# One call instead of two for the second query tile's scores in a fused attention and mixture-of-experts kernel

## What is computed

```python
att = jnp.einsum('bhqd,bhkd->bhqk', q, k) * jnp.float32(SCALE)
allowed = _sliding_window_mask(t, W)          # (j <= i) & (j >= i - window + 1)
att = jnp.where(allowed[None, None], att, jnp.float32(-jnp.inf))
att = jax.nn.softmax(att, axis=-1)
out = jnp.einsum('bhqk,bhkd->bhqd', att, v)
...
x = _layernorm(x + _L0_attn_ref(x, L0_attn_w_qkv, L0_attn_w_out), axis=-1)
x = _layernorm(x + _L0_ffn_ref(x, ...), axis=-1)
```

## Time and profile before

| | |
|---|---|
| median of 3 runs | 224.28 us (223.73 to 225.29) |
| the profiled execution, its own time | 223.83 us |
| its span, first to last instruction | 221.8 us |
| around the span | 2.0 us |
| PE busy / weight loads | 203.4 us (92%) / 135.9 us |
| DVE busy | 182.9 us (82%) |
| ACT busy | 116.7 us (53%) |
| POOL busy | 89.2 us (40%) |
| mean granted TensorE clock | 0.960 |

### The profile page before, as it was taken

How to read it: one execution, slowest core, us unless ns; L and a number is a source line. 1 busy time by engine, 2 the same in 40 slices (tenths; PEclk the granted TensorE clock), 3 DMA queues, 4 the chain that set the end, 5 groups by cost and what they waited for, 6 DMA issues and landing times.

```text
span 221.8 us, 5963 instructions
## 1 busy us (share of the span) xinstructions
PE 203.4 (92%) x1906; PEld 135.9 (61%) x1908; DVE 182.9 (82%) x522; ACT 116.7 (53%) x270; POOL 89.2 (40%) x166
## 2 busy tenths in 40 slices
PE   7786999989999999999999999989999899999960
PEld 4332446555565565565566566656688798989950
DVE  6664655789979989989989998977899888988883
ACT  2200106647557557557557566769445756374530
POOL 7230003375445635635635536478244211422103
PEclk9997559999999999999999999999999999999996
DMA  4947751542633533533533431000000001000011
GB/s 113 282 117 240 202 148 46 151 147 77 170 120 104 163 110 99 162 104 99 160 104 99 158 104 29 5 26 3 0 4 0 0 3 45 7 24 24 3 47 47
DMA packets 20391, 19.66 MB, mean 89 GB/s; under 512 B 1609, under 2 KB 17937, under 8 KB 20369
## 3 DMA queue, kind: packets, MB, share of 16 engines
q1 hardware_dynamic: 20180, 19.30, 29.4%
q10 hardware_dynamic: 189, 0.09, 0.1%
HBM read 13.94 MB, written 5.24 MB: 86 GB/s over the span
## 4 chain that ended last, share of the span: by engine, by line
PE 63%; DVE 17%; issue 7%; ACT 4%; DMA 4%; POOL 1%; SPq 1%; DVEq 1%; POOLq 0%; ACTq 0%
PE bank L1051 12%; PE bank L1043 9%; PE bank L960 7%; PE bank L977 5%; PE bank L992 4%; PE bank L955 3%; PE bank L942 3%; PE bank L945 3%; PE bank L926 3%; PE bank L1089 3%; DMA ks<-k_scratch 2%; DVE rest L671 2%; DVE neg_max L748 2%; PE bank L978 2%; DVE parts L676 2%
## 5 line engine op out<-in xcount | busy, mean ns | idle before, releaser
L474 ACT ACTIVATE probs<-bank 128x384 f32<-128x384 f32 x128 | 60.0, 496 | 34.7 <-PE bank L978 32.5
L432 POOL TENSOR_SCALAR_AFFINE_SELECT probs<-probs 128x1024 f32<-128x1024 f32 x32 | 35.7, 1116 | 67.8 <-ACT probs L474 67.8
L813 DVE SCALAR_TENSOR_TENSOR x_rows<-bank,gate_c,x_rows 128x128 f32<-128x128 f32 (+1 forms) x128 | 36.6, 343 | 5.3 <-PE bank L1051 4.2
L748 DVE TENSOR_REDUCE neg_max<-bank 128x2 f32<-128x384 f32 x64 | 33.5, 546 | 3.4 <-PE bank L960 3.1
L1051 PE MATMUL bank<-w_out_sb,hid 128*128 128x128 f32 x256 | 34.2, 277 | 1.0 <-DVE x_rows L813 1.0
L1051 PEld LDWEIGHTS bank<-w_out_sb,hid 128*128 128x128 f32 x256 | 32.6, 191 | 3.4 <-DVE x_rows L813 1.4
L574 ACT ACTIVATE hid<-bank,b_in_sb 128x512 f32<-128x512 f32 x32 | 21.9, 687 | 22.4 <-PE bank L1043 22.3
L977 PE MATMUL bank<-qs,ks 75*128 75x256 bf16 x128 | 33.4, 279 | 0.1
L743 DVE TENSOR_REDUCE neg_max<-bank 128x4 f32<-128x512 f32 x32 | 21.9, 685 | 8.8 <-PE bank L945 8.1
L978 PE MATMUL bank<-qs,ks 75*128 75x128 bf16 x128 | 26.9, 218 | 0.0
L436 POOL TENSOR_SCALAR_AFFINE_SELECT probs<-probs 128x512 f32<-128x512 f32 x32 | 24.2, 756 | 0.0
(11 more groups left out here) (117 smaller groups left out, 343.8 us busy)
## 6 DMA issues: line engine op xcount, KB each, us to landing
qs<-q_scratch SPq DMA_DIRECT2D x16, 288.0 KB
ks<-k_scratch SPq DMA_DIRECT2D x16, 288.0 KB
q_scratch<-parts SPq DMA_DIRECT2D x8, 192.0 KB, 2.1
k_scratch<-parts SPq DMA_DIRECT2D x8, 192.0 KB, 2.4
x_cols<-x_t SPq DMA_DIRECT2D x8, 128.0 KB, 2.6
x_rows<-x SPq DMA_DIRECT2D x8, 128.0 KB, 2.2
k_scratch<-parts SPq DMA_DIRECT2D x8, 128.0 KB, 2.3
out<-y_sb SPq DMA_DIRECT2D x8, 128.0 KB, 1.8
```

What stands on the lines that cost most here:

```text
L432: pool.affine_select(out=own, in_=own, compare_op=ALU.is_ge, fill=0.0, base=0, pattern=[[0, 2], [0, 4], [1, P]], channel_multiplier=-1).th ...
L474: nc.scalar.activation(probs[g][:, :, i, :], st_banks(spare)[k % len(st_banks(spare))][:, 0:3 * P].rearrange("p (k c) -> p k c", k=3), ACT ...
L748: nc.vector.tensor_reduce(neg_max[:, 1, 4 * g + 2 * u:4 * g + 2 * u + 2], score_bank[1 + u][:, 0:384].rearrange("p (h c) -> p h c", h=2), ...
L813: nc.vector.scalar_tensor_tensor(token_rows(c, n), y_bank[e % 4][:, n * E:(n + 1) * E], gate_of(c, n, e), token_rows(c, n), ALU.mult, ALU. ...
```

## The change

The function takes both u at once. It issues both waits and both mask products, then all eight 64-column products. It stands where the call for u = 0 stood, ahead of `turned_scores` i = 1; the call for u = 1, ahead of `turned_scores` i = 2, is gone. Number and form of the products are the same as before.

```diff
-            def scores_second_tile(b, g, u, in_use):
+            def scores_second_tile(b, g, in_use):
 
                 q, k = qs[b.parity][g // 2], ks[b.parity][g // 2]
-                bank_u = score_bank[1 + u]
-                if in_use:
-                    pe.wait_ge(maxima, b.times(3 * QUADS, 3 * g - (1 - u)))
-                edges = bank_u[:, 0:384].rearrange("p (h a c) -> p h a c", h=2, a=3)[:, :, 0:3:2, :]
-                mm(edges, ident_bf[:, :], mask_second[:, :, :].unsqueeze(1).to_broadcast([P, 2, 2, 64]), start=True, stop=True)
-                for i in range(2):
-                    h = 4 * (g % 2) + 2 * u + i
-                    for half in range(2):
-                        lo = 64 * half
-                        last = mm(bank_u[lo:lo + 64, i * 192:(i + 1) * 192], q[0:ROWS, h, P + lo:P + lo + 64], k[0:ROWS, h, lo:lo + 192],
-                                  start=False, stop=True, skip_group_check=True)
-                last.then_inc(scores_ready, 1)
+                for u in range(2):
+                    if in_use:
+                        pe.wait_ge(maxima, b.times(3 * QUADS, 3 * g - (1 - u)))
+                    edges = score_bank[1 + u][:, 0:384].rearrange("p (h a c) -> p h a c", h=2, a=3)[:, :, 0:3:2, :]
+                    mm(edges, ident_bf[:, :], mask_second[:, :, :].unsqueeze(1).to_broadcast([P, 2, 2, 64]), start=True, stop=True)
+                for u in range(2):
+                    for i in range(2):
+                        h = 4 * (g % 2) + 2 * u + i
+                        for half in range(2):
+                            lo = 64 * half
+                            last = mm(score_bank[1 + u][lo:lo + 64, i * 192:(i + 1) * 192], q[0:ROWS, h, P + lo:P + lo + 64],
+                                      k[0:ROWS, h, lo:lo + 192], start=False, stop=True, skip_group_check=True)
+                    last.then_inc(scores_ready, 1)
...
-                        scores_second_tile(s, g, 0, in_use)
+                        scores_second_tile(s, g, in_use)
...
-                    if on["score"]:
-                        scores_second_tile(s, g, 1, in_use)
```

## The result

| | before | after |
|---|---|---|
| median of 4 runs each | 224.70 us (223.73 to 225.29) | 238.39 us (235.37 to 244.31) |
| ratio of the two | | 1.0532, 95% interval 1.0417 to 1.0647 |
| the profiled execution, its own time | 223.83 us | 235.37 us |
| its span | 221.8 us | 233.4 us |
| mean granted clock | 0.960 | 0.933 |

The forecast was 227.7 us in a range of 224.6 to 230.5. The sign was right, the size was not: 13.7 us by the medians where 3.4 were forecast.

A forecast was written before the change was run, and what follows sets the result against it. A step was taken as a ring: `project_qk` to group 1's mask, 5.00 us by ACT and DVE, then 11.57 us of PE's list; 0.2 + 0.93 + 2.0 + 0.5 - 0.2 = +3.4 us gave 227.7 us, 80% within 224.6 to 230.5.

The forecast's parts named there:

- The place of the wait: Group 1, steps 1 to 6: the second mask waits for the reduction of group 0, u = 1, 1.5 to 2 us.
- rival B: Group 0: DVE's last splitting step goes ahead of POOL's masking, `project_qk` to mask 0.76 us shorter; total 223.9; chance 0.2.
- Rival C: Group 1: PE's wait costs nothing, mode changes alone count; 32 groups x 0.17 = 5.4 us gained, 218.9; chance 0.04.
- the second arc: PE's list from group 1's mask product of u = 1 to the next `project_qk`, 11.57 us, with 0.26 us visible wait.
- Group 1: +0.94: Group 1: work now behind the wait, 0.89 us, plus 0.05 for `turn_output` reached later.
- 0.17 us saved in a group: PE, each group: both masks and eight products take 0.83 us against 2 x 0.50; saving between 0.10 and 0.21.
- The other groups of a step: Groups 2 and 3 save 0.17 us each, L1026's wait saves 0.26, the next group 0 costs 0.33.
- the 0.26 us at L1026: PE's wait for DVE's `normalise`, 0.26 us a step, expected to go because PE comes there 0.8 us later.
- -0.43: Group 2's first mask to `turn_x1`: 0.17 us saved by merging and 0.26 us of wait at L1026 gone.
- the forecast 0.67: One loop step's added time: 0.94 - 0.34 - 0.26 + 0.33 = +0.67 us.
- The granted clock is 1.00 from 34 us to the experts' end: PE: no fall of the clock in the changed kernel between 34 us and the end of the experts.
- rival D: PE's new idle time in group 1 halves the clock: once 233 us, in every step 250 and more; chance 0.1.

The follow-up runs named there:

- The two experiments on group 2: Added in turn to the change with seven idle products: transfer L515 issued earlier, 228.87 us; group 2's merged call behind `turned_scores` i = 1, 226.95 us.

## Why the prediction was right in sign and wrong in size

**The place of the wait, right.** The mask product of u = 1 waits for (0,1) in steps 1 to 6, for 1.6 to 1.8 us, 4.9 to 5.05 us after `project_qk` (in step 5 for 0.9 us, 4.23 us after it: rival B below). The kernel with the wait alone, the one with two unmerged calls and the one with DVE's reduction first show that it is this wait, and nothing of the merging, that costs. Rival C, which needed air in the second arc, is ruled out.

**"Group 1: +0.94", right.** Measured 0.95, in the kernel with the idle products.

**"0.17 us saved in a group", a little small.** The call takes 0.77 us (87.84 to 88.61), not 0.83, so 0.23 are saved. The pair distance was taken as 0.11, from inside a call, where it is (0.77 - 0.21 - 0.29 - 0.11) / 2 = 0.08, close to the 0.09 of streaming. The upper end of the stated saving, 0.21, was the better one. That a change of the tiling mode drains TensorE stands in the Trainium skill, TensorEngine Tiling (Array Packing), Tiling Modes; the trace agrees in kind, since 0.23 us are saved with half of the mode changes, but doesn't tell the drain from a shorter pair distance.

**"The other groups of a step", failed at group 2.** The prediction took off 0.17 and the 0.26 us at L1026, and stated that ACT, POOL and SP keep their order. They keep it, but not their times: the exponential i = 1 of group 1 comes 6.04 us after `project_qk` instead of 4.43, as the prediction's own 104.2 says, the transfer that ACT issues beside it too, and `turned_scores` i = 0 of group 2, itself only 0.95 us later, needs that transfer. I had followed that issue to the copies of v and not to who waits for the data. And the removed call had stood between `turned_scores` i = 1 and 2 (as the code shows, in every group), giving ACT 0.5 us; without it PE waits for the exponential. In place of -0.43 stands +0.27. The two experiments on group 2 took 0.55 and 0.26 us off the step and leave 0.47, which is near the forecast 0.67.

**"The granted clock is 1.00 from 34 us to the experts' end", failed.** The prediction took the full clock as the likeliest and gave rival D 0.1, with a price of 5 us for one stretch and a total of 250 us and more if every step had one. What happened lies between: stretches of 3.4 to 6.8 us behind four of six waits. They cost about 7.6 us by the medians of the two kernels with and without the idle products. "Open from where it decides" was true of the trace of before, and with an interval from 0.71 us (nothing) to 2.76 us (a stretch of 13.65 us), six new idle times of 1.8 us lay in the upper half of the unknown; the chance of 0.1 was too low for that, and the range, which ended at 230.5, left it out.

**Rival B, partly right.** L676 took 0.69 us in one of the steps of the kernel after (timelines of DVE and POOL):

```profile
109.61 0.69 DVE L676 TENSOR_TENSOR parts<-rest,parts 128x512 bf16<-128x512 f32 x1
109.63 1.63 POOL L432 TENSOR_SCALAR_AFFINE_SELECT probs<-probs 128x1024 f32<-128x1024 f32 x1
```

DVE was first by 0.02 us. The wait at L955 was 0.89 there and the step 17.00 instead of 17.82. The other steps kept POOL first. With the merged call at the second place DVE was first in steps 3 to 6.

**Sum.** The order of the work costs 6.2 us by the medians of the kernel with the idle products, where 3.4 were forecast. In its profiled execution steps 1 to 5 are 1.52, 1.56, 1.24, 1.29 and 0.50 us longer than before, 6.1 in all, where the forecast has 3.1 up to there (0.2 + 0.93 + 2.0); in step 5 DVE was first, by 0.01 us. Only step 4 was taken apart, and its excess is group 2's. What lies behind the sixth `project_qk` is 1.8 us longer, where 0.3 was forecast, and the start 3.5 shorter, with 6.8 us less at half clock; neither was tested by itself. The clock costs the other 7.6.

## What to carry to other kernels

When a wait moves ahead of other work on a full engine, price not only the work behind it but each transfer that is issued next to what it delays, up to the one who reads it. And count new idle time of TensorE apart, by length: here waits of some 1.3 to 1.9 us, once every 17 us, cost about as much through the clock as the new order of the work did, and a few idle products in the wait took that part back. Of two places for a merged call the later one, where its last input is nearly there, was the one that gained.

## What was not expected of the hardware

The clock's answer to an idle time is neither sure nor of one length. Over all profiled executions, between 33 and 141 us, PE had 18 waits of 1.29 to 1.99 us and 17 of 0.89 to 1.25. Behind 13 of the 18 the clock fell within 2.0 us, behind five it did not (1.78, 1.66, 1.37, 1.36 and one of three of 1.29); behind one of the 17 it fell (1.17, while 1.18 and 1.25 passed). Most stretches lasted 3.4 us, one of them, behind 1.39 us, 23.9, though PE was busy throughout. What decides between these was not found.

DVE's L676 (512 bf16 elements a partition from two f32 inputs) takes 0.69 us when it starts 0.01 to 0.33 us ahead of POOL's masking L432, and 1.46 to 1.55 us when POOL is ahead by 0.09 to 0.41 us; POOL's own time is 1.1 us when it is ahead by up to 0.2, and 1.5 to 1.6 when DVE is ahead by 0.01 to 0.15. A tenth of a microsecond in the order of two engines that share no data decide over 0.8 us of the chain. The ends fit one blocking the other: in the earlier trace rows L676 ends 0.54 us behind the end of L432 (102.62 and 102.08), and at the second place L432 ends 0.96 us behind the end of L676 (85.35 and 84.39), in both cases about what the second one takes alone, less 0.15. By the Trainium skill, SBUF — State Buffer, section Who interferes with whom, a DVE instruction with two inputs in SBUF contends with a GpSimd instruction that reads SBUF, and the port pair that they share is an exclusive lock. L676 and L432 are such a pair, and the trace agrees, but for these 0.15 us.
